# Moving the shared part of the key projection u ahead of a query product in an attention-and-MLP kernel

## The reference

```
q_hk   = (layernorm(x) @ Wq.T).reshape(B, S, H, K)
q_big  = rope(einsum('bshk,hkq->bshq', q_hk, w_kc_q))        # 192 wide
kv_r   = rope(kv_c)                                          # 64 wide
q_r    = einsum('bshq,hqr->bhsr', q_big, W_qr)
k_r    = einsum('bld,hdr->bhlr', kv_r, W_kr)
attn   = softmax(einsum('bhsr,bhlr->bhsl', q_r, k_r))
ctx_c  = einsum('bhsl,bld->bhsd', attn, kv_r)
x     += (einsum('bhsd,hkd->bhsk', ctx_c, w_kc_kv) as S x HK) @ Wo.T
```

## Time and profile before

| | us |
|---|---|
| median of 3 runs | 395.29 |
| lowest and highest of them | 394.91, 396.79 |
| the profiled execution | 395.89 |
| its span, first to last instruction | 394.1 |

### The profile page before, as it was taken

The page is one execution under the profiler, slowest core; times in us unless marked ns, Lnnn a source line. Parts: engine busy times, 40 slices in busy tenths (PEclk is TensorE's granted clock), DMA queues, the critical chain, the costliest instruction groups (busy, mean ns, idle before and its releaser), DMA issues.

```text
span 394.1 us, 6266 instructions
## 1 busy us (share of the span) xinstructions
PE 371.5 (94%) x2121; PEld 261.5 (66%) x2121; DVE 305.5 (78%) x676; ACT 216.7 (55%) x564; POOL 180.2 (46%) x170
## 2 busy tenths in 40 slices
PE   7899999999999999999999999987799897999996
PEld 7766677676766776767666787742265454778885
DVE  5697698697866986778778583778989998897673
ACT  1525466546654766566645875337889232573250
POOL 2554576457645764576447403945700062055100
PEclk9999999999999999999999999999958999999999
DMA  7639000301103003000040002100000000000001
GB/s 233 221 109 371 14 2 0 107 2 38 72 0 108 2 1 107 2 0 2 1 148 0 2 0 74 44 2 0 1 0 2 0 0 2 1 0 2 27 28 54
DMA packets 9087, 17.54 MB, mean 45 GB/s; under 512 B 2144, under 2 KB 6944, under 8 KB 8160
## 3 DMA queue, kind: packets, MB, share of 16 engines
q1 hardware_dynamic: 9056, 17.14, 12.8%
HBM read 16.09 MB, written 1.05 MB: 43 GB/s over the span
## 4 chain that ended last, share of the span: by engine, by line
PE 69%; DVE 18%; ACT 5%; POOL 3%; DMA 2%; issue 2%; SPq 0%; DVEq 0%
PE bank L1524 16%; PE bank L1595 8%; PE bank L1570 7%; PE bank L1586 6%; PE bank L1616 6%; PE bank L1554 4%; PE bank L1539 3%; PE bank L1476 3%; DVE relu L1153 2%; PE bank L1443 2%; PE bank L1765 2%; DMA blobs<-in_blob 2%; PE bank L1444 1%; PE bank L1445 1%; PE bank L1483 1%
## 5 line engine op out<-in xcount | busy, mean ns | idle before, releaser
L456 POOL TENSOR_TENSOR prob<-prob,rinv 128x512 f32<-128x512 f32 x64 | 65.9, 1041 | 74.5 <-DVE rinv L1023 74.5
L1524 PE MATMUL bank<-xnT,w 128*128 128x512 f32 x288 | 90.2, 434 | 1.7 <-DVE xnT L921 1.7
L618 ACT ACTIVATE prob<-bank,negmax 128x256 f32<-128x256 f32 x128 | 59.3, 481 | 29.5 <-DVE negmax L1017 29.5
L1017 DVE TENSOR_REDUCE negmax<-bank 128x2 f32<-128x512 f32 x64 | 40.9, 682 | 36.5 <-PE bank L1570 36.5
L1524 PEld LDWEIGHTS bank<-xnT,w 128*128 128x128 f32 x288 | 50.3, 189 | 19.5 <-issue 13.3
L628 ACT COPY probT<-bank 128x512 f32<-128x512 f32 x64 | 37.8, 591 | 22.6 <-PE bank L1586 22.1
L952 DVE TENSOR_TENSOR rot_up<-bank,cb 64x512 f32<-64x512 f32 x64 | 44.1, 689 | 1.6
L451 POOL TENSOR_TENSOR rot_low<-rot_low,rot_up 128x512 f32<-128x512 f32 x32 | 40.9, 1279 | 3.8 <-DVE rot_up L952 3.8
L436 POOL TENSOR_TENSOR c_y<-c_ve,minus_half 128x4 f32<-128x4 f32 (+1 forms) x9 | 9.8, 1088 | 65.8 <-DVE c_ve L902 52.7
L1586 PE MATMUL bank<-ca,prob 128*128 128x128 f32 x256 | 39.4, 276 | 0.5 <-ACT probT L628 0.3
L1586 PEld LDWEIGHTS bank<-ca,prob 128*128 128x128 f32 x256 | 29.1, 140 | 13.8 <-issue 5.6
(11 more groups left out here) (210 smaller groups left out, 715.7 us busy)
## 6 DMA issues: line engine op xcount, KB each, us to landing
blobs<-in_blob SPq DMA_DIRECT2D x7, 1024.0 KB, 4.9
xs<-in_x SPq DMA_DIRECT2D x2, 512.0 KB, 4.0
xn<-in_w_fc_t SPq DMA_DIRECT2D x1, 1024.0 KB, 4.9
ctxT<-in_w_proj_t SPq DMA_DIRECT2D x1, 1024.0 KB, 5.5
out<-qk SPq DMA_DIRECT2D x8, 128.0 KB, 1.7
cb<-in_const_b SPq DMA_DIRECT2D x1, 768.0 KB, 8.8
blobs<-in_w_gate SPq DMA_DIRECT2D x1, 704.0 KB, 4.3
blobs<-in_w_up SPq DMA_DIRECT2D x1, 704.0 KB, 5.6
```

What stands on the lines that cost most here:

```text
L456: pool.tensor_tensor(p[:], p[:], rinv[:, n % PROBS, :].unsqueeze(2).to_broadcast([P, 2, S]), ALU.mult).then_inc(normed, 1)
L618: ins = act.activation(prob[n % PROBS][:, st, :], pS[n % UNITS][:, st * S:(st + 1) * S], ACT.Exp, bias=negmax[:, n % UNITS, st:st + 1], ac ...
L1017: dve.tensor_reduce(negmax[:, n % UNITS, :], pS[n % UNITS][:].rearrange("p (a s) -> p a s", a=2), AX, ALU.max, negate=True).then_inc(max_r ...
L1524: ins = pe.matmul(q_bank(m)[:], w[a][:, k, r * P:(r + 1) * P], x[b][:, k, c * CH:(c + 1) * CH], start=(i == 0), stop=(i == 5))
```

## The change

In each of the 14 rounds of the loop, PE's list has the shared part of u of the next round directly behind the scores, and tile m's six query matmuls behind it; before, the query matmuls came first. No instruction is added or removed, no wait is changed, and no other engine's list is touched.

```diff
                 n, m = UNITS * g, RT * (g + 2)
                 first, second = folds_at(g)
                 small_tiles(g)
+                latent_u(g + 1, 1)
                 latent_q(m)
-                latent_u(g + 1, 1)
                 latent_q_part(m + 1, 0, 2)
                 turn_probs(n)
                 latent_q_part(m + 1, 2, 6)
```

## The result

The changed kernel takes 403.62 us (median of 4 runs, 403.34 to 403.77), against 395.38 for the kernel before in the same session: a ratio of 1.0215, 95% interval 1.0197 to 1.0234, 8.2 us slower. The forecast was 405.3, in a range of 401.5 to 407.2.

What follows compares the result with a forecast made beforehand. PE was taken to bound the kernel, busy 13.01 of 13.10 us in round 6. Losses of 7.6 + 0.85 + 0.86 + 0.65 = 10.0 us on the 395.29 median gave 405.3 us, range 401.5 to 407.2.

Steps and rivals of the forecast that it cites:

- the loss comes by way of DVE's list and POOL: In the loop, late tile m delays DVE's rotation and inverse sum, then POOL, then PE's fourth-unit weight load: 0.69 us a round.
- the shared part costs PE nothing by itself and gains nothing: On PE behind the scores, starting 1.59 us earlier: cost nothing, gain nothing or 1.5 us at most, taken as nothing.
- The terms of the sum: Loop losses: 7.6 us in rounds 1 to 11, 0.85 behind round 0, 0.86 in round 12, 0.65 in round 13.
- plain delay: From POOL's end of the fourth unit's normalising to PE's weight load: 0.12 us, read from round 12.
- rounds 1 to 11: PE's fourth-unit load starts at t = 9.72 instead of 9.03: 0.69 us lost in each of 11 rounds, 7.6 in all.
- 0.04 to spare: At PE's fourth-unit weight load in round 6, POOL's answer came just in time, with 0.04 us of room.
- rival of a hidden delay: No change, 395.3 us, if PE had 0.69 us of room at the fourth-unit weight load; chance 0.03.
- Round 12: No weight piece fills the time and PE already waits for the fourth unit, so POOL's delay counts: 0.86 us lost.
- Rounds 0 and 13: Behind round 0 POOL's whole delay counts, 0.85 us; round 13 loses 0.74 at most, taken as 0.65.
- The rule of the Trainium skill on short stops between groups of matmuls: PE's short waits could make the loop's clock go up and down; one round at half clock gives 418 us, chance 0.04.
- about 216 ns from one 512-column matmul to the next: For the shared part's two matmuls: tile m only 0.43 us late, sum some 4 us; as rival 399.2 us, chance 0.04.
- the 0.68 us wait of the earlier trace: In round 13 PE's next step waited 0.68 us for a DVE constant; DVE was taken to be late by 0.55 only.

Runs made afterwards that it cites:

- experiment 1: The changed kernel with DVE's inverse sums of the second and third unit moved ahead of tile m's straight and first crossed rotation: 396.28 us, ratio 1.0031.
- experiment 2: The changed kernel with only the second unit's inverse sum moved ahead of the straight rotation on DVE: 402.59 us, ratio 1.0184.
- experiment 4: The kernel before with the shared part between the third and fourth of tile m's six query matmuls: 404.43 us, ratio 1.0237.
- experiment 5: The kernel before with the shared part cut into two column halves, one directly behind the scores, one behind tile m's query matmuls: 398.15 us, ratio 1.0081.
- experiment 7: The kernel before with the shared part two matmuls later, behind the first two of tile m+1: 395.43 us, ratio 1.0015.
- Experiment 6: The changed kernel with POOL's normalising of the fourth unit moved ahead of its first join: 402.01 us, ratio 1.0179.

## Why the prediction was right, and where its size was off

**That the loss comes by way of DVE's list and POOL** is shown: experiment 1 takes it away without touching PE, experiment 2 moves it by one unit, experiment 4 makes it without the new place, experiment 5 gives the amount that the same chain gives for half the lateness.

**That the shared part costs PE nothing by itself and gains nothing** holds: 2.45 us for the two steps in either order; ACT's copy waits as often as before; experiment 7.

**The terms of the sum.** The rotation, the inverse sum and POOL's normalising came at t = 4.48, 5.08 and 5.32, each as worked out. Too large was the step from POOL's end to PE's load, the "plain delay" of 0.12 from round 12: in the changed kernel POOL ends at 124.49 + 1.04 = 125.53 and the load starts at 125.58, 0.05 later. So rounds 1 to 11 lose 0.61 and not 0.69, 6.7 us instead of 7.6; this is the term that was mis-sized.

Behind it stands a misreading of who released that load in the kernel before. The code has it wait for two things: POOL's normalising of its own unit, and ACT's copy of the transposes of the unit before (both use one PSUM tile). The timeline of the kernel before, round 6 and then round 12, shows ACT's copy ending last or at the same time:

```profile
120.19 0.59 ACT L628 COPY probT<-bank 128x512 f32<-128x512 f32 x1 [0.36 <-PE bank L1586]
```

```profile
198.25 1.05 POOL L456 TENSOR_TENSOR prob<-prob,rinv 128x512 f32<-128x512 f32 x1
...
198.72 0.59 ACT L628 COPY probT<-bank 128x512 f32<-128x512 f32 x1 [0.81 <-PE bank L1586]
```

In round 6 ACT ends at 120.78 and POOL at 120.73, and the load starts at 120.89; in round 12 they end at 199.31 and 199.30, and it starts at 199.42. In all of rounds 1 to 12 the load starts 0.11 or 0.12 after ACT's copy, while POOL's end lies anywhere from 0.12 to 0.31 ahead of it. In the changed kernel it starts 0.05 or 0.06 after POOL's end in every round, with ACT's copy 0.39 us or more ahead. Experiment 6 parts the two furthest: in its rounds 12 and 13 POOL ends 0.43 ahead of the load, and ACT's copy 0.10 and 0.11, as ever. So before the change it was ACT that released this load, though the profile names POOL, and 0.12 was not POOL's delay. The prediction's "0.04 to spare" in round 6 was 0.11 (0.16 − 0.05), the room that experiment 5 also shows. Its rival of a hidden delay, which asked for 0.69 of room here, had a part of it. The row for POOL's own delay was at hand: in round 13 of the kernel before, where POOL ends last, the load follows it by 0.05:

```profile
211.26 1.04 POOL L456 TENSOR_TENSOR prob<-prob,rinv 128x512 f32<-128x512 f32 x1
...
212.35 0.42 PEld L1586 LDWEIGHTS bank<-ca,prob 128*128 128x128 f32 x4 [0.50 <-POOL prob L456]
```

Round 12 lost 0.74 instead of 0.86. POOL's second join did end 0.86 later (t = 10.84 instead of 9.98), but before, PE came to its next step only at t = 10.15, 0.17 behind POOL, since a weight piece stood in between (L1487 at 200.01, behind the fourth unit); now it comes to it 0.05 behind POOL, at t = 10.89. The prediction had counted round 12 as one without a weight piece. Rounds 0 and 13 lost 0.84 and 0.62, for 0.85 and 0.65.

**Outside the loop** the sum had nothing, and the profiles differ by 1.08 us in favour of the changed kernel. Of the 1.7 us by which the median is under the forecast, 1.1 are the terms above; the rest lies out here. Most of the difference of the profiles is in the stretch behind the loop. Late in the kernel the granted clock falls to 0.50 (1.2 GHz) in both: before the change as a stop of PE of 2.04 us ends, in the changed kernel some 3 us behind the same stop. It stays there for some 14 us in the one and some 7 in the other. Windows of the kernel before and, in the fence below it, of the changed one (stretch, us, busy by engine, granted clock, DMA):

```profile
284.00:288.00 4.00, 3.69 (x9) 2.52 (x10) 2.59 (x15) 1.18 (x3) 0.00 (x0) 0.53 0.00 0
...
296.00:298.00 2.00, 2.00 (x7) 0.73 (x5) 1.76 (x4) 2.00 (x3) 0.00 (x0) 0.52 0.00 0
298.00:300.00 2.00, 2.00 (x14) 1.27 (x13) 1.97 (x3) 2.00 (x5) 0.00 (x0) 1.00 0.00 0
```

```profile
294.00:296.00 2.00, 1.40 (x8) 0.92 (x7) 1.35 (x9) 0.07 (x1) 0.00 (x0) 1.00 0.00 0
296.00:298.00 2.00, 2.00 (x7) 1.58 (x6) 1.50 (x2) 2.00 (x2) 0.00 (x0) 0.53 0.00 0
...
302.00:304.00 2.00, 2.00 (x13) 1.26 (x11) 1.97 (x3) 2.00 (x3) 0.00 (x0) 0.76 0.00 0
```

The code there is the same in all nine profiles, and the stretch from the scores of round 14 to the end goes with the mean clock of the profile, whichever the kernel: 176.4 to 176.7 us in the three with a mean of 0.991 or 0.992, 177.1 to 177.7 in the six with 0.979 to 0.985. Kernels with the order of the change are in both groups, and one run of the kernel before with a mean clock of 0.991 is on record as well (394.11 us, beside experiments 5 to 7), though without a trace. So I count this part as a difference between executions, and not as the change's; no run here shows what makes the stretch longer or shorter.

**The clock in the loop.** PE stands idle in each changed round now, and the granted clock of round 6, as of the whole loop, is still 1.00:

```profile
115.94:129.65 13.71, 13.38 (x82) 8.85 (x80) 9.69 (x19) 8.08 (x25) 7.82 (x7) 1.00 0.14 39
```

The rule of the Trainium skill on short stops between groups of matmuls ("TensorE: Matmul & The Clock Gate", section "A second HAM failure mode: psum-queue depth-cycling"), by which the clock could have gone up and down, did not come true with 0.33 us of idle PE in 13.71, nor with 1.20 in the 13.62 of round 13. The other rule of that page, about 216 ns from one 512-column matmul to the next by its formula for an isolated one ("Back-to-back issue gap"), would by estimate have made the change as cheap as experiment 5, if it held for these f32 operands; the rows give the shared part 0.86 us for its two instructions, and the measurement decides.

## What to carry to other kernels

Moving a step forward in an in-order list moves all that it passes back. Before asking who waits for the step that goes forward, ask who takes the results of the steps that are passed, and what stands behind that taker in its own list: here a rotation on DVE that was wanted only later held up the inverse of two numbers a row, on which POOL and PE waited. Where a late operand can't be avoided, the small urgent instruction goes ahead of the large one that has to wait: with two small lines of DVE's list moved up, the same order on PE cost 0.3% instead of 2%. And where an instruction waits for two others that end close together, the profile can name the wrong one: look over several rounds at which of the two distances stays the same.

## What the runs showed of the hardware that was not expected

A DVE instruction on two columns, L1071 (a tensor_scalar, 128x2, operands in SBUF), took 1.16 us in the kernel before and 0.17 in the changed one; its neighbour L1065 took 1.13 and 0.23. The kernel before, then the changed one, in the timeline of round 13:

```profile
212.25 1.26 POOL L451 TENSOR_TENSOR rot_low<-rot_low,rot_up 128x512 f32<-128x512 f32 x1
...
212.39 1.16 DVE L1071 TENSOR_SCALAR wsi<-wsi 128x2 f32<-128x2 f32 x1
```

```profile
221.37 0.17 DVE L1071 TENSOR_SCALAR wsi<-wsi 128x2 f32<-128x2 f32 x1
221.43 1.27 POOL L451 TENSOR_TENSOR rot_low<-rot_low,rot_up 128x512 f32<-128x512 f32 x1
```

Where POOL's join had already started, the DVE instruction ended with it, at 213.55 and 213.51; where it started 0.06 ahead of the join, it took 0.17. The line is a fine one: in experiment 2 L1065 started 0.02 ahead of a join and was held as well, for 1.31 us, to 0.03 after its end. DVE's reciprocals on two columns were not held that way: one took 0.17 while POOL ran (116.07 in the first experiment's fence). The Trainium skill, "GPSIMD Engine Reference", section "Specifications", says that POOL and DVE share SBUF interfaces, and that DVE's instructions in a two-port mode or with two SBUF inputs contend for them; the rows fit that, but no run here tells which of the two this instruction is. It made the 0.68 us wait of the earlier trace rows, which is gone in the changed kernel (PE now waits there for POOL's second join, 0.57 us).
